# Pairing the head groups, the butterflies and x2's halves of an attention layer on Trainium2, and reordering VectorE's queue

## The chip, the cores and the metric

The kernel runs on one core of a Trainium2 chip. The core has TensorE (PE, matrix products, which read SBUF and write PSUM), VectorE (DVE), ScalarE (ACT), GpSimd (POOL, which has no way to PSUM) and SyncE (SP, which here only issues DMAs). Each engine has its own queue of instructions and works through it strictly in order; between engines only semaphores order the work, and a wait at the head of a queue holds everything behind it. The metric is the device time of the whole program in microseconds (us): the median of the runs of the kernel before is 1216.87 us (three runs, 1216.46 to 1218.15).

## The reference

```
x: (8, 1024, 512) f32; 16 heads of 32
a = layernorm(x)
Q, K, V = a@Wq.T+bq, a@Wk.T+bk, a@Wv.T+bv           (split into heads)
S = Q K^T / sqrt(32) - |i - j|, causal               (decay of the distance, -inf above the diagonal)
x = x + layernorm(softmax(S) V @ Wo.T + bo)
h = layernorm(x) @ Hadamard(512)                     (orthonormal)
q = round(h / s) * s,  s = max|h| / 7 of a row, clipped to 4 bits
x = x + layernorm(q @ ternary(W).T)
```

Because the decay is one per key of distance, a query only needs keys a short way back; the kernel computes the keys of its own 256 tokens and 64 or so before them, and checks on the chip that the inputs allow this (a flag selects a general path otherwise, which is not executed here).

## The kernel before

The 8192 tokens are cut into 32 steps of 256 (two token tiles of 128; four steps make one of the 8 sequences). The loop is a software pipeline over steps: while step s weighs its values, the queues also hold the projections of step n = s+1, the layernorm of m = s+2, the output product and the first residual of k = s-1, and the quantised product of k-1 = s-2. The order inside a step is written out by hand, once for each engine.

Large products are made in f16 with both factors split into a high and a low part (high*high + low*high + high*low, helper `split_product`, L1264). So every intermediate that goes into such a product is made twice: ACT copies it to f16 (the high part), and DVE or POOL subtracts that from the f32 value (the low part).

What the change touches:

- The 16 heads of a step are handled as four groups g = 0..3 of four heads. `keys(s, g, half)` on PE makes the scores, `exps` on ACT their exponentials, `clear_future(s, g)` on POOL (L458) zeroes what lies after the query, and `weigh(s, g)` on PE (L1380, L1385) writes into PSUM bank `ps_o[g % 2]` the weighted values (columns 0 to 255) and the sums of the weights (columns 256 to 511). Then `invert(s, g)` on ACT makes the reciprocal of the sums as exp(-ln) (L629, L631), `normalise(s, g)` on DVE multiplies and takes one Newton step in three instructions (L953, L955, L958), each waiting for the one before, into `o32[:, g % 2]`, `heads_high(s, g)` on ACT (L636) and `heads_low(s, g)` on POOL (L464) split the result into `OT`. `out_product` needs all four groups.
- `weigh(s, g)` waits until `normalise` of two groups before has read its bank. In the loop, PE weighs groups 0 and 1 in mid-step, group 2 late in the step, between the second product of V `values(n, 1)` and the third block of `scores`, and group 3 at the start of the following step, between `qk(n, 0)` and `qk(n, 1)`.
- The Hadamard transform of 512 is done as two butterflies on DVE (`fold`, L994 and L995; `fold_again`, L1003 and L1004) and a product with a 128x128 Hadamard matrix on PE (`transform`, L1407). `x2_high` (ACT, L642) and `x2_low` (DVE, L1017) split the folded rows, `turn_x2` (SP, L327) transposes both parts by DMA. All of this is done for each of the two token tiles by itself: 8 butterfly instructions, 2 + 2 splits and 4 DMA transposes a step.
- Four PSUM banks `ps_job` are taken in turn by the jobs listed in `ORDER`; a job begins when the job before it in the same bank has been read (`claim`). Thus `values(n, 1)` waits for `scale_out(k - 1, 1)` on DVE (L1041), the third and fourth block of `scores(n, ...)` (L1336, L1338) for `maxima(n, 0)` and `maxima(n, 1)` on DVE (L931), `qk(n+1, 0)` for `keep_norms(n)` (L923), `qk(n, 3)` for `qk_low_part(n, 1)` (L917) and `out_product(k, 0)` for `qk_low_part(n, 2)`.
- `residual(k)` (DVE, L987) needs the root of the variance that POOL computes in `y_root` (L446) from `y_stats` (DVE).

DVE's order in a step before, from the second `y_out` on: `y_out(k, 1)`, `y_stats(k)`, `normalise(s, 0)`, `residual(k)`, `scale_out(k-1, 0)`, the eight butterflies, `scale_out(k-1, 1)`, `z_stats(k-1)`, `x2_low(k, 0)`, `normalise(s, 1)`, `maxima(n, 0)`, `maxima(n, 1)`, `keep_norms(n)`, `z_columns(k-1)`, `x2_low(k, 1)`, `maxima(n, 2)`, `maxima(n, 3)`, `split_max(n)`, `normalise(s, 2)`, `x_stats(k)`; then of the following step `qk_low_part(n, 0)`, `normalise(k, 3)`, `qk_low_part(n, 1)`, `front_stats(m)`, `find_scale(k-1, 0)`, `front_offset(m)`, `qk_low_part(n, 2)`, `find_scale(k-1, 1)`, `qk_low_part(n, 3)`, `y_out(k, 0)`, `front_low(m)`.

Of the kernel before, what the change touches and what calls it, by code (L numbers as in the profile page):

```python
# [5 lines left out]
P = 128  # L6
# [27 lines left out]
TP = 2  # L34
# [32 lines left out]
def fast_path(nc, x, wqT, wkT, wvT, woT, bq, bk, bv, bo, wff, had16, identity, window, ident16,  # L67
# [3 lines left out]
    with ExitStack() as ctx:  # L71
# [10 lines left out]
        ps_o = [ps("o0"), ps("o1")]  # L82
# [9 lines left out]
        def score_bank(n, i):  # L92

            return bank("s", i) if n else (ps_st + ps_o)[i]
# [137 lines left out]
        x2_turned = [sem(f"x2_turned{t}") for t in range(TP)]  # L232
# [59 lines left out]
        def _(sp):  # L292
# [107 lines left out]
            for s in range(STEPS - 1):  # L400
# [14 lines left out]
                if has(k):  # L415
                    turn_x2(k, 0)
                    turn_x2(k, 1)
# [4 lines left out]
            turn_x2(last - 1, 0)  # L422
            turn_x2(last - 1, 1)
            load_res(last)
            turn_x2(last, 0)
            turn_x2(last, 1)

        @block.gpsimd
        def _(pool):
# [32 lines left out]
            def heads_low(s, g):  # L462
                pool.wait_ge(OTh_made, 4 * s + g + 1)
                nc.gpsimd.tensor_tensor(OT[s % 2][1][:, g, :], o32[:, g % 2, :], OT[s % 2][0][:, g, :],  # L464
                                        ALU.subtract).then_inc(OTl_made, 1)
# [21 lines left out]
            for s in range(STEPS - 1):  # L487
                n, m, k = s + 1, s + 2, s - 1
                square_of(n, 0)
                if has(k):  # L490
                    heads_low(k, 3)
                if has(m):
                    front_root(m)
                if has(n):
                    square_of(n, 1)
                if has(s):
                    clear_future(s, 0)
                    clear_future(s, 1)
                if has(k):
                    y_root(k)  # L500
                if has(s):
                    clear_future(s, 2)
                if has(k - 1):
                    z_root(k - 1)
                if has(s):
# [5 lines left out]
                if has(s):  # L511
                    heads_low(s, 2)

            last = STEPS - 1
            heads_low(last - 1, 3)
# [4 lines left out]
            heads_low(last, 0)  # L520
            clear_future(last, 3)
            z_root(last - 2)
            heads_low(last, 1)
            heads_low(last, 2)
            heads_low(last, 3)
# [13 lines left out]
        def _(act):  # L539
# [85 lines left out]
            def invert(s, g):  # L625

                act.wait_ge(pv_done, 4 * s + g + 1)
                until(act, o32_made, 4 * s + g - 1)
                nc.scalar.activation(inverse[:, g % 2, :], ps_o[g % 2][:, W2:D], ACT.Ln).then_inc(log_made, 1)  # L629
                act.wait_ge(log_made, 4 * s + g + 1)  # L630
                nc.scalar.activation(inverse[:, g % 2, :], inverse[:, g % 2, :], ACT.Exp,  # L631
                                     scale=-1.0).then_inc(inverse_made, 1)

            def heads_high(s, g):
                act.wait_ge(o32_made, 4 * s + g + 1)
                nc.scalar.activation(OT[s % 2][0][:, g, :], o32[:, g % 2, :],  # L636
                                     ACT.Copy).then_inc(OTh_made, 1)

            def x2_high(k, t):
                act.wait_ge(folded, 2 * (TP * k + t) + 2)  # L640
                until(act, q_turned, TP * (k - 1) + t + 1)
                nc.scalar.activation(x2h[:, t, :], folded_x[:, t, :], ACT.Copy, scale=SX).then_inc(x2h_made, 1)  # L642
# [43 lines left out]
            for s in range(STEPS - 1):  # L686
                n, m, k = s + 1, s + 2, s - 1
                qk_high_part(n, 0)
                if has(k):
                    invert(k, 3)  # L690
# [3 lines left out]
                if has(k):  # L694
                    heads_high(k, 3)
# [24 lines left out]
                invert(s, 0)  # L720
                exps(s, 2, 0)
                invert(s, 1)
# [4 lines left out]
                if has(k):  # L727
# [4 lines left out]
                exps(s, 3, 1)  # L732
                keep_v(n, 1)
# [8 lines left out]
            invert(last - 1, 3)  # L742
            heads_high(last - 1, 3)
# [9 lines left out]
            invert(last, 0)  # L753
            exps(last, 2, 0)
            keep_q(last - 2, 1)
            exps(last, 2, 1)
            exps(last, 3, 0)
            invert(last, 1)
            heads_high(last, 0)
            x2_high(last - 1, 0)  # L760
            exps(last, 3, 1)
            x2_high(last - 1, 1)
            invert(last, 2)
            heads_high(last, 1)
            norm_z(last - 2)
            invert(last, 3)
            heads_high(last, 2)
            heads_high(last, 3)
# [6 lines left out]
            x2_high(last, 0)  # L775
            x2_high(last, 1)
# [10 lines left out]
        def _(dve):  # L787
# [159 lines left out]
            def normalise(s, g):  # L947

                dve.wait_ge(inverse_made, 4 * s + g + 1)

                until(dve, OTl_made, 4 * s + g - 1)
# [133 lines left out]
            for s in range(STEPS - 1):  # L1085
                n, m, k = s + 1, s + 2, s - 1
                qk_low_part(n, 0)
                if has(k):
                    normalise(k, 3)
# [37 lines left out]
                if has(k):  # L1127
                    x2_low(k, 0)
# [4 lines left out]
                if has(k - 1):  # L1133
                    z_columns(k - 1)
# [994 lines left out]
```

## Time and profile before

| | |
|---|---|
| median of the runs shown | 1216.87 us |
| the profiled execution | 1216.83 us, span 1215.3 us |
| busy, share of the span | PE 91%, DVE 83%, weight loads 60%, ACT 58%, POOL 49% |
| granted TensorE clock, mean of the span | 0.974 |

The profile comes from one execution, 1216.83 us, of which 1215.3 us lie within the span; the other 1.5 us lie around it. The program begins with the load of the weights (until about 40 us in) and ends with a drained pipeline (from about 1110 us on); in between it is a loop whose steps take about 35 us each. Matmuls overlap one another, so a start-to-start distance says more of PE's pace than a duration does; the same is true of DVE and ACT, where the next instruction begins before the recorded end of the one before.

### The profile page before, as it was taken

To read this page: it belongs to the slowest core of one execution; us is meant where nothing else is said; L and a number is where in the kernel's file an instruction comes from. 1 tells how busy PE (TensorE), PEld (TensorE's weight loads), DVE (VectorE), ACT (ScalarE), POOL (GpSimd) and SP (SyncE) were. 2 spreads that over 40 slices of the span, in tenths; PEclk is the share of its full clock that TensorE was granted. 3 is DMA by queue.
4 is the path that set the end of the run, shared out by engine and by line. 5 is a ranking of instruction groups with operands and counts; after the bars stand their busy time and mean duration, and the time that the engine had idled before them with its cause. 6 is when DMAs were issued, how large, how long until landed. Compare 5 with 4: busy or idle time off the path is not lost.

```text
span 1215.3 us, 44904 instructions
## 1 busy us (share of the span) xinstructions
PE 1105.3 (91%) x18656; PEld 728.3 (60%) x18656; DVE 1009.3 (83%) x2558; ACT 702.9 (58%) x1494; POOL 595.7 (49%) x715
## 2 busy tenths in 40 slices
PE   5899999999999999999999999999999999999641
PEld 3566556666666666666566666666666666666320
DVE  5748998888988888899888888988888899887772
ACT  5454556665566566655666666556666655665431
POOL 2233545555454556555545555454556555545422
PEclk9999999999999999999999999999999999999875
DMA  9657565665666576656665655666576657654230
GB/s 270 150 119 143 113 138 137 155 133 132 144 124 137 138 149 145 131 132 145 124 139 137 159 135 135 137 127 134 148 139 151 135 127 151 123 115 104 67 70 37
DMA packets 204817, 161.83 MB, mean 133 GB/s; under 512 B 150432, under 2 KB 150688, under 8 KB 204512
## 3 DMA queue, kind: packets, MB, share of 16 engines
q1 hardware_dynamic: 199920, 141.86, 55.1%
q0 software_dynamic: 4688, 17.04, 3.9%
q8 instruction: 149, 2.44, 0.9%
q14 instruction: 60, 0.49, 0.1%
HBM read 40.87 MB, written 16.78 MB: 47 GB/s over the span
## 4 chain that ended last, share of the span: by engine, by line
PE 57%; DVE 31%; issue 7%; ACT 2%; SPq 1%; DMA 1%; POOL 1%; POOLq 0%; DVEq 0%; ACTq 0%
PE f_job L1264 42%; DVE f_bst L963 6%; PE f_st L1363 3%; DVE f_z L1041 3%; PE f_o L1380 2%; PE f_o L1385 2%; PE f_job L1407 2%; DVE f_o L953 2%; DVE f_inverse L955 2%; DVE f_x L987 2%; DVE f_rmax L931 2%; DVE f_folded_x L1004 2%; DVE f_y L995 2%; DVE f_y L994 2%; DVE f_small L989 1%
## 5 line engine op out<-in xcount | busy, mean ns | idle before, releaser
L458 POOL TENSOR_SCALAR_AFFINE_SELECT f_PT<-f_PT 64x512 f32<-64x512 f32 (+1 forms) x256 | 201.0, 809 | 69.6 <-ACT f_PT L618 44.2
L473 POOL TENSOR_TENSOR f_square<-f_stage 128x512 bf16<-128x512 f16 x128 | 130.9, 1044 | 135.4 <-ACT f_stage L596 119.6
L596 ACT ACTIVATE f_stage<-f_job,f_bias 128x256 f16<-128x256 f32 x256 | 106.1, 465 | 88.6 <-PE f_job L1264 81.7
L1264 PE MATMUL f_job<-f_xTh,f_wqh 128*128 128x256 f16 x512 | 140.8, 275 | 15.1 <-DVE f_wkl L794 14.3
L464 POOL TENSOR_TENSOR f_OTl<-f_o,f_OTh 128x256 f16<-128x256 f32 x128 | 86.1, 673 | 115.1 <-ACT f_OTh L636 114.5
L1264 PE MATMUL f_job<-f_xTl,f_wqh 128*128 128x256 f16 x512 | 140.1, 274 | 0.0
L1264 PE MATMUL f_job<-f_xTh,f_wql 128*128 128x256 f16 x512 | 140.1, 274 | 0.0
L1264 PE MATMUL f_job<-f_xTh,f_wkh 128*128 128x256 f16 x512 | 140.0, 273 | 0.0
L1264 PE MATMUL f_job<-f_xTh,f_wkl 128*128 128x256 f16 x512 | 139.9, 273 | 0.0
L1264 PE MATMUL f_job<-f_xTl,f_wkh 128*128 128x256 f16 x512 | 139.8, 273 | 0.0
L917 DVE SCALAR_TENSOR_TENSOR f_stage<-f_job,f_bias,f_stage 128x256 f16<-128x256 f32 x256 | 110.7, 474 | 31.7 <-ACT f_stage L596 29.7
L450 POOL TENSOR_TENSOR f_small<-f_small,f_minus_half 128x2 f32<-128x2 f32 x32 | 33.4, 1043 | 179.0 <-DVE f_small L1051 178.9
L1264 PE MATMUL f_job<-f_wvh,f_xTh 128*128 128x512 f16 x256 | 98.5, 385 | 20.1 <-DVE f_z L1041 19.3
L618 ACT ACTIVATE f_PT<-f_st 128x512 f32<-128x512 f32 x192 | 106.5, 599 | 10.0 <-PE f_st L1363 10.0
L604 ACT ACTIVATE f_V<-f_job 128x512 f32<-128x512 f32 x64 | 38.3, 598 | 112.5 <-PE f_job L1264 112.5
L1264 PE MATMUL f_job<-f_woh,f_OTh 128*128 128x512 f16 x256 | 99.2, 387 | 0.3 <-POOL f_OTl L464 0.3
L1363 PEld LDWEIGHTS f_st<-f_stacks 128*64 128x64 f16 x2432 | 67.8, 111 | 51.5 <-issue 40.0
L1264 PE MATMUL f_job<-f_woh,f_OTl 128*128 128x512 f16 x256 | 98.5, 385 | 0.0
L1264 PE MATMUL f_job<-f_wvh,f_xTl 128*128 128x512 f16 x256 | 98.3, 384 | 0.0
L1264 PE MATMUL f_job<-f_wol,f_OTh 128*128 128x512 f16 x256 | 98.3, 384 | 0.0
L1264 PE MATMUL f_job<-f_wvl,f_xTh 128*128 128x512 f16 x256 | 98.2, 384 | 0.0
L973 DVE SCALAR_TENSOR_TENSOR f_y<-f_job,f_bo_bc 128x512 f32<-128x512 f32 x64 | 44.2, 691 | 64.9 <-PE f_job L1264 64.9
(180 smaller groups left out, 3033.3 us busy)
## 6 DMA issues: line engine op xcount, KB each, us to landing
f_stacks<-f_stage SPq DMA_DIRECT2D x384, 128.0 KB
f_xin<-x SPq DMA_DIRECT2D x32, 512.0 KB, 4.7
f_x<-x SPq DMA_DIRECT2D x32, 512.0 KB, 3.9
out<-f_z POOLq DMA_DIRECT2D x32, 512.0 KB, 3.4
f_Vmix<-f_V SPq DMA_DIRECT2D x32, 256.0 KB
f_Vmix<-f_V SPq DMA_DIRECT2D x64, 128.0 KB
f_stacks<-rows_const SPq DMA_DIRECT2D x3, 512.0 KB, 9.3
f_stacks<-wqT SPq DMA_DIRECT2D x2, 512.0 KB, 5.8
```

Of the source, the lines that this page charges most:

```text
L458: nc.gpsimd.affine_select(out=d, in_=d, compare_op=ALU.is_ge, fill=0.0, base=odd * SUB, pattern=[[0, 4], [0, TP], [1, SUB]], channel_multi ...
L464: nc.gpsimd.tensor_tensor(OT[s % 2][1][:, g, :], o32[:, g % 2, :], OT[s % 2][0][:, g, :], ALU.subtract).then_inc(OTl_made, 1)
L473: nc.gpsimd.tensor_tensor(square[:, 2 * m + pair, :], h, h, ALU.mult).then_inc(squared, 1)
L596: nc.scalar.activation(stage[:, 2 * m, g, :], bank("qk", g)[:, m * W2:(m + 1) * W2], ACT.Identity, bias=bias[:, m, g:g + 1]).then_inc(qk_h ...
L604: nc.scalar.activation(V[n % 2][:, t, :], bank("v", t)[:], ACT.Copy, scale=1.0 / SQ).then_inc(v_kept, 1)
L618: nc.scalar.activation(dst, src, ACT.Exp, scale=1.0 / SS).then_inc(expd, 1)
L917: nc.vector.scalar_tensor_tensor(stage[:, 2 * m + 1, g, :], bank("qk", g)[:, m * W2:(m + 1) * W2], bias[:, m, g:g + 1], stage[:, 2 * m, g, ...
L963: note(nc.vector.bn_stats(bst[:, which, t, :], src[:, t, :]))
L973: nc.vector.scalar_tensor_tensor(y[:, t, :], bank("y", t)[:], -1.0 / (SQ * SW), bo_bc[:], ALU.mult, ALU.add).then_inc(y_made, 1)
L1041: nc.vector.tensor_tensor(z[:, t, :], bank("f", t)[:], ffscale_bc[:], ALU.mult).then_inc(z_made, 1)
L1264: mm = pe.matmul(dst, lhs[a](c), rhs[b](c), start=(n == 0), stop=(n == 3 * KC - 1))
L1363: mm = pe.matmul(ps_st[half][upper * SUB:(upper + 1) * SUB, i * W2 + q * SUB:i * W2 + (q + w) * SUB], Ks[js % 3][:, h, c * SUB:(c + 1) * SUB],
```

## The change

Groups are inverted, normalised and split two at a time: `invert`, `normalise`, `heads_high` and `heads_low` take a width w, and one instruction covers two groups (the two banks of `ps_o` become one tensor of two banks). `weigh(s, 2)` moves out of its place before the third block of scores to the following step, directly ahead of `weigh(s, 3)`. The butterflies, `x2_high`, `x2_low` and the DMA transposes of x2 cover both token tiles in one instruction. The orders of all five queues are adapted; on DVE `normalise(s, 0)` no longer stands between `y_stats` and `residual`, and groups 0 and 1 are normalised after `keep_norms` and `x2_low`. In the last step groups 2 and 3 are still handled one by one.

```diff
-        ps_o = [ps("o0"), ps("o1")]
+        ps_pair = ctx.enter_context(nc.psum_tensor("f_o", [P, 2, D], F32))
+        ps_o = [ps_pair[:, i, :] for i in range(2)]
@@ SP
-            def turn_x2(k, t):
-                sp.wait_ge(x2l_made, TP * k + t + 1)
-                until(sp, h_product, TP * (k - 1) + t + 1)
+            def turn_x2(k):
+                until(sp, h_product, TP * k)
                 for half, src in enumerate((x2h, x2l)):
-                    sp.dma_start(x2T[half][:, t], src[:, t, :], transpose=True).then_inc(x2_turned[t], 16)
+                    sp.wait_ge((x2h_made, x2l_made)[half], k + 1)
+                    sp.dma_start(x2T[half][:].rearrange("p t c n -> p (t c) n"),
+                                 src[:].rearrange("p t n -> p (t n)"), transpose=True).then_inc(x2_turned, 16)
@@ POOL
-            def heads_low(s, g):
-                pool.wait_ge(OTh_made, 4 * s + g + 1)
+            def heads_low(s, g, w):
+                pool.wait_ge(OTh_made, 4 * s + g + w)
+                nc.gpsimd.tensor_tensor(OT[s % 2][1][:, g:g + w, :], o32[:, g % 2:g % 2 + w, :],
+                                        OT[s % 2][0][:, g:g + w, :], ALU.subtract).then_inc(OTl_made, w)
...
                 square_of(n, 0)
-                    heads_low(k, 3)
+                    heads_low(k, 2, 2)
...
                     y_root(k)
-                    clear_future(s, 2)
+                clear_future(s, 2)
+                clear_future(s, 3)
                     z_root(k - 1)
-                    clear_future(s, 3)
-                    heads_low(s, 0)
-                    heads_low(s, 1)
+                heads_low(s, 0, 2)
                     finish_out(k - 1)
-                    heads_low(s, 2)
@@ ACT
-            def invert(s, g):
-                act.wait_ge(pv_done, 4 * s + g + 1)
-                until(act, o32_made, 4 * s + g - 1)
+            def invert(s, g, w):
+                slots = slice(g % 2, g % 2 + w)
+                act.wait_ge(pv_done, 4 * s + g + w)
+                until(act, o32_made, 4 * s + g + w - 2)
+                nc.scalar.activation(inverse[:, slots, :], ps_pair[:, slots, W2:D], ACT.Ln).then_inc(log_made, w)
+                act.wait_ge(log_made, 4 * s + g + w)
+                nc.scalar.activation(inverse[:, slots, :], inverse[:, slots, :], ACT.Exp,
+                                     scale=-1.0).then_inc(inverse_made, w)
...
-                    invert(k, 3)
+                    invert(k, 2, 2)
...
-                    heads_high(k, 3)
+                    heads_high(k, 2, 2)
...
-                invert(s, 0)
                 exps(s, 2, 0)
-                invert(s, 1)
+                invert(s, 0, 2)
                     keep_q(k - 1, 1)
                 exps(s, 2, 1)
                 keep_v(n, 0)
-                    x2_high(k, 0)
-                    x2_high(k, 1)
-                heads_high(s, 0)
                 exps(s, 3, 0)
                 exps(s, 3, 1)
+                    x2_high(k)
                 keep_v(n, 1)
+                heads_high(s, 0, 2)
                     norm_z(k - 1)
-                invert(s, 2)
-                heads_high(s, 1)
-                heads_high(s, 2)
@@ DVE
+            def normalise(s, g, w):
+                slots = slice(g % 2, g % 2 + w)
+                dve.wait_ge(inverse_made, 4 * s + g + w)
+                until(dve, OTl_made, 4 * s + g + w - 2)
+                heads, sums, inv = ps_pair[:, slots, 0:W2], ps_pair[:, slots, W2:D], inverse[:, slots, :]
+                nc.vector.tensor_tensor(heads, heads, inv, ALU.mult).then_inc(o_scaled, w)
+                dve.wait_ge(o_scaled, 4 * s + g + w)
+                nc.vector.tensor_tensor(inv, sums, inv, ALU.mult).then_inc(o_error, w)
+                dve.wait_ge(o_error, 4 * s + g + w)
+                nc.vector.scalar_tensor_tensor(o32[:, slots, :], inv, 2.0, heads,
+                                               ALU.subtract, ALU.mult).then_inc(o32_made, w)
...
+            def fold(k):
+                dve.wait_ge(x1_made, TP * k + TP)
+                left, right = x1[k % 2][:, :, 0:W2], x1[k % 2][:, :, W2:D]
+                nc.vector.tensor_tensor(y[:, :, 0:W2], left, right, ALU.add).then_inc(halved, 1)
+                nc.vector.tensor_tensor(y[:, :, W2:D], left, right, ALU.subtract).then_inc(halved, 1)
...
-                    normalise(k, 3)
+                    normalise(k, 2, 2)
...
-                normalise(s, 0)
                     residual(k)
                     scale_out(k - 1, 0)
-                    fold(k, 0)
-                    fold_again(k, 0)
-                    fold(k, 1)
-                    fold_again(k, 1)
+                    fold(k)
+                    fold_again(k)
                     scale_out(k - 1, 1)
                     z_stats(k - 1)
-                    x2_low(k, 0)
-                normalise(s, 1)
                 maxima(n, 0)
                 maxima(n, 1)
                 keep_norms(n)
+                    x2_low(k)
+                normalise(s, 0, 2)
                     z_columns(k - 1)
-                    x2_low(k, 1)
                 maxima(n, 2)
                 maxima(n, 3)
                 split_max(n)
-                normalise(s, 2)
                     x_stats(k)
...
-                pe.wait_ge(x2_turned[t], 32 * (k + 1))
+                pe.wait_ge(x2_turned, 32 * (k + 1))
@@ PE
                     qk(n, 0)
+                    weigh(k, 2)
                     weigh(k, 3)
                     qk(n, 1)
...
                 values(n, 1)
-                weigh(s, 2)
                 scores(n, 2)
                 scores(n, 3)
```

In the last step DVE now has `normalise(last, 0, 2)` where `normalise(last, 0)` stood (between `y_stats(last-1)` and `residual(last-1)`), and `fold(last)`, `fold_again(last)`, `x2_low(last)` over both tiles.

## Rows read from the trace of the kernel before

**Rows 1.** The page's first part, busy time of each engine:

```profile
PE 1105.3 (91%) x18656; PEld 728.3 (60%) x18656; DVE 1009.3 (83%) x2558; ACT 702.9 (58%) x1494; POOL 595.7 (49%) x715
```

**Rows 2.** Waits of PE, 100 to 1100 us: total us, times, longest:

```profile
PE f_job L1264 <- DVE f_z L1041: 18.5, 27, 1.9
PE f_job L1336 <- DVE f_rmax L931: 7.2, 13, 0.6
PE f_job L1338 <- DVE f_rmax L931: 3.9, 7, 0.6
PE f_job L1336 <- DMA f_stacks<-f_stage: 1.2, 3, 0.5
```

**Rows 3.** Timeline of PE, one step: start, us, instruction [idle before]:

```profile
409.71 0.32 PE L1380 MATMUL f_o<-f_PT,f_Vmix 128*32 128x64 f32 x8
...
410.61 0.29 PE L1380 MATMUL f_o<-f_PT,f_Vmix 128*32 128x64 f32 x8
...
419.25 0.39 PE L1264 MATMUL f_job<-f_wvh,f_xTh 128*128 128x512 f16 x1 [0.81 <-DVE f_z L1041]
...
421.94 0.32 PE L1380 MATMUL f_o<-f_PT,f_Vmix 128*32 128x64 f32 x8
...
423.58 0.19 PE L1336 MATMUL f_job<-f_stacks 107*32 107x24 f16 x1 [0.55 <-DVE f_rmax L931]
...
424.71 0.28 PE L1264 MATMUL f_job<-f_xTh,f_wqh 128*128 128x256 f16 x1
...
427.43 0.32 PE L1380 MATMUL f_o<-f_PT,f_Vmix 128*32 128x64 f32 x8
...
428.45 0.28 PE L1264 MATMUL f_job<-f_xTh,f_wqh 128*128 128x256 f16 x1
...
437.96 0.39 PE L1264 MATMUL f_job<-f_woh,f_OTh 128*128 128x512 f16 x1
...
459.54 0.28 PE L1264 MATMUL f_job<-f_xTh,f_wqh 128*128 128x256 f16 x1
```

**Rows 4.** Timeline of DVE, the same step:

```profile
409.46 0.69 DVE L973 SCALAR_TENSOR_TENSOR f_y<-f_job,f_bo_bc 128x512 f32<-128x512 f32 x1 [1.13 <-PE f_job L1264]
...
411.87 0.43 DVE L953 TENSOR_TENSOR f_o<-f_o,f_inverse 128x256 f32<-128x256 f32 x1
...
413.13 1.41 DVE L987 SCALAR_TENSOR_TENSOR f_x<-f_y,f_small,f_x 128x512 f32<-128x512 f32 x2
...
415.59 0.41 DVE L994 TENSOR_TENSOR f_y<-f_x 128x256 f32<-128x256 f32 x1
...
418.51 0.68 DVE L1041 TENSOR_TENSOR f_z<-f_job,f_ffscale_bc 128x512 f32<-128x512 f32 x1
...
422.91 1.15 DVE L931 TENSOR_REDUCE f_rmax<-f_job 128x8 f32<-128x448 f32 x2
...
424.57 0.15 DVE L1055 TENSOR_TENSOR f_small<-f_small 128x2 f32<-128x2 f32 x1
...
436.27 0.87 DVE L917 SCALAR_TENSOR_TENSOR f_stage<-f_job,f_bias,f_stage 128x256 f16<-128x256 f32 x2
```

**Rows 5.** Timeline of POOL, the root that `residual` waits for:

```profile
412.04 0.70 POOL L446 TENSOR_TENSOR f_small<-f_small,f_minus_half 128x2 f32<-128x2 f32 x1 [1.95 <-DVE f_small L979]
```

**Rows 6.** Timeline of ACT, the end of the same step:

```profile
424.95 1.52 ACT L662 ACTIVATE f_z<-f_z,f_small 128x512 f32<-128x512 f32 x2 [2.30 <-DVE f_small L1057]
```

**Rows 7.** Groups of DVE by form, 100 to 1100 us: busy us, mean ns:

```profile
L973 DVE SCALAR_TENSOR_TENSOR f_y<-f_job,f_bo_bc 128x512 f32<-128x512 f32 x56 | 38.7, 691 | 48.0 <-PE f_job L1264 48.0
...
L1041 DVE TENSOR_TENSOR f_z<-f_job,f_ffscale_bc 128x512 f32<-128x512 f32 x56 | 38.1, 680 | 0.0
```

**Rows 8.** Timeline of SP's queue, the regrouping of Q and K:

```profile
440.23 9.66 SPq L353 DMA_DIRECT2D f_stacks<-f_stage  x12
```

**Rows 9.** Timeline of PE and of DVE in the drained end:

```profile
1161.85 0.59 PE L1264 MATMUL f_job<-f_woh,f_OTh 128*128 128x512 f16 x1 [0.32 <-POOL f_OTl L464]
...
1184.08 0.16 DVE L1026 SCALAR_TENSOR_TENSOR f_job<-f_x_mv,f_job 128x1 f32<-128x1 f32 x1
```

More of the change, by code:

```diff
@@ L231, in fast_path @@
         folded = sem("folded")
-        x2_turned = [sem(f"x2_turned{t}") for t in range(TP)]
+        x2_turned = sem("x2_turned")
         x2h_made = sem("x2h_made")
@@ L415, in _ @@
                 if has(k):
[L416 to L417 removed]
+                    turn_x2(k)
             last = STEPS - 1
@@ L519, in _ @@
             clear_future(last, 2)
-            heads_low(last, 0)
+            z_root(last - 2)
             clear_future(last, 3)
[L522 to L525, printed above, removed]
+            heads_low(last, 0, 2)
+            heads_low(last, 2, 1)
+            heads_low(last, 3, 1)
             finish_out(last - 2)
@@ L752, in _ @@
             level(last - 2, 1)
-            invert(last, 0)
             exps(last, 2, 0)
+            invert(last, 0, 2)
             keep_q(last - 2, 1)
@@ L757, in _ @@
             exps(last, 3, 0)
-            invert(last, 1)
-            heads_high(last, 0)
-            x2_high(last - 1, 0)
             exps(last, 3, 1)
-            x2_high(last - 1, 1)
-            invert(last, 2)
-            heads_high(last, 1)
+            heads_high(last, 0, 2)
+            x2_high(last - 1)
+            invert(last, 2, 1)
             norm_z(last - 2)
-            invert(last, 3)
-            heads_high(last, 2)
-            heads_high(last, 3)
+            invert(last, 3, 1)
+            heads_high(last, 2, 1)
+            heads_high(last, 3, 1)
             round_levels(last - 1, 0)
@@ L774, in _ @@
             keep_q(last - 1, 1)
-            x2_high(last, 0)
-            x2_high(last, 1)
+            x2_high(last)
             norm_z(last - 1)
@@ L1144, in _ @@
             last = STEPS - 1
-            normalise(last - 1, 3)
+            normalise(last - 1, 2, 2)
             find_scale(last - 2, 0)
@@ L1150, in _ @@
             y_stats(last - 1)
-            normalise(last, 0)
+            normalise(last, 0, 2)
             residual(last - 1)
@@ L1154, in _ @@
             scale_out(last - 2, 1)
-            fold(last - 1, 0)
-            fold_again(last - 1, 0)
+            fold(last - 1)
+            fold_again(last - 1)
             z_stats(last - 2)
-            fold(last - 1, 1)
-            fold_again(last - 1, 1)
-            x2_low(last - 1, 0)
-            normalise(last, 1)
+            x2_low(last - 1)
             z_columns(last - 2)
-            x2_low(last - 1, 1)
-            normalise(last, 2)
-            normalise(last, 3)
+            normalise(last, 2, 1)
+            normalise(last, 3, 1)
             x_stats(last - 1)
@@ L1172, in _ @@
             residual(last)
-            fold(last, 0)
-            fold_again(last, 0)
-            fold(last, 1)
-            fold_again(last, 1)
-            x2_low(last, 0)
+            fold(last)
+            fold_again(last)
+            x2_low(last)
             scale_out(last - 1, 0)
             scale_out(last - 1, 1)
-            x2_low(last, 1)
             z_stats(last - 1)
@@ L1491, in _ @@
             last = STEPS - 1
+            weigh(last - 1, 2)
             weigh(last - 1, 3)
```

86 lines of the change are left out of this document (28 added, 58 removed).

## The prediction

> **What bounds the kernel now.** The first view is busy time: PE 91% of the span, DVE 83%, the others far behind [rows 1]. PE is the candidate, but its share is an average, so the next view is who makes PE wait. In 1000 us of the loop it waited 29.6 us for DVE, at three places: before `values(n, 1)` for `scale_out` (18.5), before the third and fourth block of scores for `maxima` (7.2 and 3.9); DMAs hardly count [rows 2]. The timeline of one step shows where: 0.81 us at 419.25 and 0.55 at 423.58 [rows 3]. The step lasts 459.54 - 424.71 = 34.83 us [rows 3]. So the loop is bound by PE's own work, with DVE late at two points of each step. DVE in turn waits for PE once, at the second `y_out` (1.13 us at 409.46, [rows 4]). The step is therefore two rings that touch: PE's queue, and DVE's queue from `y_out(k, 1)` round to `qk_low_part(n, 2)`, which frees the bank of the next output product (PE at 437.96). I work out both for the new order; the longer one is the new step.
>
> **DVE's ring.** Before, `y_out(k, 1)` at 409.46 to `qk_low_part(n, 2)` at 436.27 is 26.81 us [rows 4].
> - Residual: `normalise(s, 0)` costs 413.13 - 411.87 = 1.26 us there [rows 4]. It goes from this place, but it covered POOL's root, which runs 412.04 to 412.74 [rows 5]. Residual can start at about 412.80, so only 0.33 us is won; DVE stands idle 0.9 us in its place.
> - Butterflies: eight take 418.51 - 415.59 = 2.92 us [rows 4]. A joined one has 512 elements a partition; the nearest row is 680 ns, for 128x512 in f32 [rows 7], and as a next instruction starts some 0.08 us before a recorded end (413.13 + 1.41 is 414.54, and eight butterflies of 0.41 take 2.92, less than 3.3), I take 0.60 start to start. Four of these and one wait of 0.11: 2.51, 0.41 won. Bound: if the joined one costs as two (0.67), 0.13 is won, not 0.41.
> - Normalising: four singles of 1.26 are 5.04 us a step. A pair is three instructions on 2x256 elements that wait for one another. The trace has no instruction over two banks; the nearest row is 691 ns for 512 elements from one bank [rows 7], the other end is two singles, 0.85 for each. With 0.69: 0.72 + 0.72 + 0.60 = 2.04 a pair, 4.08 a step. Since the first single is already counted under residual, three singles (3.78) become two pairs (4.08): +0.30. With the other end +1.26.
> - `x2_low`, 2 x 0.60 against one of about 1.22: nothing. An idle 0.17 ahead of `qk_low_part(n, 1)`, where ACT was late, is used up.
> - Sum: -0.33 - 0.41 + 0.30 - 0.17 = -0.61, so 26.20. The `qk_low` itself takes 0.87 [rows 4]; from the output product at 437.96 round to the next `y_out(k, 1)` are 34.83 - (437.96 - 409.46) = 6.33 [rows 3, 4], pure PE work. Ring: 26.20 + 0.87 + 0.05 + 6.33 = 33.45 us.
>
> **PE's ring.** Its two waits go as causes: 34.83 - 0.81 - 0.55. `weigh(s, 2)` moves. Alone between f16 products a weigh occupies 423.58 - 0.55 - 421.94 = 1.09 and 428.45 - 427.43 = 1.02; the first of two in a row takes 410.61 - 409.71 = 0.90 [rows 3]. Two together are then 0.90 + 1.02 = 1.92, not 2.11: 0.19 won. That makes 33.28. Now what is late next:
> - `scale_out(k-1, 1)` starts 0.33 + 0.41 earlier, 417.77, and ends at 418.50; PE is free at 419.25 - 0.81 = 418.44. 0.06 is left of the first wait.
> - `values(n, 1)` takes 421.94 - 419.25 = 2.69, then come the two score blocks, at 421.19. DVE from `scale_out` to `maxima` took 422.91 - 418.51 = 4.40, of which a single normalise and one `x2_low` (1.86) now come later: `maxima` start at 420.31 and end at 420.9 and 421.4; the blocks want them at 421.2 and 421.7. No wait. `keep_norms` follows (two maxima and it: 424.57 - 422.91 = 1.66), done at 422.05; `qk(n+1, 0)` wants it at 421.19 + 1.13 = 422.32 (424.71 - 423.58) [rows 3, 4]. No wait, by 0.3.
> - The new wait: `weigh(s, 2)` needs the whole of `normalise(s, 0, 2)`, that stands behind `x2_low`: 421.97 + 1.22 + 2.14 = 425.3. PE is there at 422.32 + 2.72 = 425.04 (427.43 - 424.71). It waits 0.3, and behind it in PE's queue are `weigh(s, 3)` and all of `qk(n, 1)`. With two-singles pairs it is 0.8.
> - PE's ring: 33.28 + 0.06 + 0.30 = 33.64, just longer than DVE's 33.45. `qk(n, 3)` finds its bank free by 0.6, the output product by 0.2.
>
> **ACT, POOL, SP.** ACT now has `heads_high(s, 0, 2)`, which waits for the pair, ahead of `norm_z` and of the next step's `qk_high_part`. `norm_z` starts at about 425.9 instead of 424.95 and takes 1.5 [rows 6]; the high part is ready by 428.2 and DVE gets to `qk_low_part(n, 0)` only at 428.7, since pair, `z_columns`, two maxima, `split_max` and `x_stats` stand before it. Nothing, as long as the pair is not over 0.5 late. POOL loses work. SP issues two long transposes for four short ones, sooner: its next waiter, `max_rows`, is not held by them. One thing does tighten: `front_offset` gives ACT its third and fourth jobs, so `qk_low_part(n, 3)`, from which the regrouping of Q and K starts, comes only 0.61 earlier a step while PE comes 1.2 earlier. The twelve transfers take up to 9.66 us to issue [rows 8], and in three steps the scores already waited for them [rows 2]. The masks of group 1 lose as much. I put both at 4 us in all, between 0 and 0.55 x 28 = 15.
>
> **The sum.** Per step of the kind shown, 34.83 - 33.64 = 1.2. Over the loop, by the waits of PE: 29.6 removed, 28 x 0.19 = 5.3 from the neighbouring weighings; new, 0.36 in three of four steps (in the first step of a sequence PE has more work and arrives later), 21 x 0.36 = 7.6, and the 4 us: 29.6 + 5.3 - 7.6 - 4 = 23.3 us. The drained end: `out_product(last, 0)` at 1161.85 hangs on the last low part [rows 9], which is as early as before; but in the last butterflies both tiles must pass ACT and DVE before `find_scale` (1184.08, [rows 9]), about 0.7 later. With less idling earlier, +0.5, between -2 and +2. 23.3 - 0.5 = 22.8. The profiled execution took 1216.83 us (span 1215.3 and 1.5 around it), as the median of the runs, 1216.87: 1216.83 - 22.8 = **1194 us**.
>
> **A rule against it.** DVE is busy 83% and leaves PE gaps of 0.81 and 0.55 us [rows 1, 3]. The Trainium skill (Perfetto Trace Analysis, Optimizing Scalar/DVE Operations) says that where such an engine isn't saturated but makes others wait, breaking instructions up may let work finish sooner. The change joins them. What this would do here is the third rival.
>
> **The rivals.**
> 1. PE runs without new waits. For it: both margins that I find negative are 0.06 and 0.3 us, the size of my errors. Against it: three engines are within 0.3 us of each other. 29.6 + 5.3 = 35 us: 1182.
> 2. Transfers and masks take what DVE gives. For it: the DMA row in [rows 2], and PE coming 0.55 us sooner on them. Against: 25 of 28 steps show no such wait. 15 us in place of 4: 1205.
> 3. The joined halves come late: PE, that needs half, waits for the whole pair. For it: the pair ends 0.9 after a single would. Then `weigh(s, 2)` waits 1.2 and not 0.3 in each step: 28 x 0.9 = 25, all the gain: 1219 at most, 1217 with the others' slack.
> 4. Slower: a joined instruction costs as its two parts. Place: DVE's ring. Price: pairs +0.96, butterflies +0.28, ACT's joined logarithm and exponential +0.35, together 1.59 us a step; 33.45 + 1.59 = 35.04, over 34.83 by 0.21, for 28 steps 6 us: 1223. It decides from 34.83 - 33.45 = 1.38 us of excess on. Against it: 512 elements cost 691 ns and not twice 430 [rows 4, 7]; for it: no row spans two banks.
>
> **Chances.** Forecast 0.60 (1186 to 1201), first rival 0.12, second 0.16, third 0.04, fourth 0.08. A measurement of this kernel tells some 0.2% (2.4 us) from no change. Faster 0.88, same 0.04, slower 0.08. The range takes in the second rival up to 1212 and the half of the first: 1183 to 1212.
>
> **What would show it.** In the profile after: steps of about 33.7 us; PE's wait for `scale_out` nearly gone, none for `maxima`, a new one of 0.3 us ahead of `weigh(s, 2)` on DVE's normalise; pairs of 0.69 us and butterflies of 0.68; an idle 0.9 us of DVE ahead of residual; the DMA wait of the scores grown. Wrong it would be if pairs take over 0.8 us, if PE waits over 1 us for DVE at the weighing, or if the output product's bank is late by more than 0.3.

## The result, and the profile after

The changed kernel takes 1245.57 us (median of four, 1244.21 to 1247.67) against 1217.41 us for the kernel before on the same chip (1216.46 to 1218.15): ratio 1.0229, 95% interval 1.0212 to 1.0245 (given so for every run below, each against the kernel before as timed beside it). It is 28 us slower where 23 us less were forecast, and outside the range.

The page of the changed kernel, busy time and the chain that ended last (line numbers are those of the changed kernel from here on):

```profile
PE 1115.3 (90%) x18625; PEld 732.8 (59%) x18656; DVE 1019.4 (82%) x2209; ACT 675.7 (54%) x1273; POOL 586.4 (47%) x652
...
DVE 60%; PE 15%; issue 10%; ACT 10%; POOL 3%; DMA 1%; SPq 1%; DVEq 0%; POOLq 0%; ACTq 0%
```

DVE runs 349 instructions fewer than before and is yet busy 10 us longer [rows 1]; DVE holds 60% of the chain, where it held 31% before. Waits of PE in the changed kernel, 100 to 1100 us (total us, times, longest), which answer to [rows 2]:

```profile
PE f_o L1350 <- DVE f_o L941: 13.7, 27, 1.0
PE f_job L1234 <- DVE f_stage L900: 12.7, 20, 0.6
PE f_job L1306 <- DVE f_rmax L914: 3.6, 8, 0.5
PE f_job L1306 <- DMA f_stacks<-f_stage: 2.9, 5, 1.1
PE f_job L1308 <- DVE f_rmax L914: 2.1, 4, 0.5
PE f_job L1306 <- issue: 1.9, 1, 1.9
PE f_job L1308 <- DMA f_stacks<-f_stage: 1.3, 2, 0.7
PE f_job L1234 <- DVE f_z L1024: 1.1, 2, 0.5
```

The wait for `scale_out` (18.5) is down to 1.1 and the new one ahead of `weigh(s, 2)` is there, as forecast; not forecast is the one before `qk(n, 3)`, for `qk_low_part(n, 1)`. So DVE is late in its long stretch from `y_out(k, 1)` on. Timeline of DVE in one step of the changed kernel, which answers to [rows 4]:

```profile
735.90 0.69 DVE L956 SCALAR_TENSOR_TENSOR f_y<-f_job,f_bo_bc 128x512 f32<-128x512 f32 x1 [0.91 <-PE f_job L1234]
...
741.22 0.68 DVE L977 TENSOR_TENSOR f_y<-f_x 128x512 f32<-128x512 f32 x1
741.81 1.14 DVE L978 TENSOR_TENSOR f_y<-f_x 128x512 f32<-128x512 f32 x1
742.99 0.69 DVE L986 TENSOR_TENSOR f_folded_x<-f_y 128x512 f32<-128x512 f32 x1
...
744.80 0.58 DVE L1029 SCALAR_TENSOR_TENSOR f_small<-f_x_mv,f_small 128x2 f32<-128x2 f32 x1
745.41 0.53 DVE L1031 SCALAR_TENSOR_TENSOR f_small<-f_small 128x2 f32<-128x2 f32 x1
...
754.09 0.61 DVE L923 TENSOR_SCALAR f_mh<-f_rmax 128x32 f16<-128x32 f32 x1
754.74 1.21 DVE L926 SCALAR_TENSOR_TENSOR f_mh<-f_rmax,f_mh 128x32 f16<-128x32 f32 x1
755.87 1.27 DVE L992 BATCH_NORM_STATS2 f_bst<-f_x 128x6 f32<-128x512 f32 x2
...
760.30 0.87 DVE L900 SCALAR_TENSOR_TENSOR f_stage<-f_job,f_bias,f_stage 128x256 f16<-128x256 f32 x2
...
771.94 0.69 DVE L956 SCALAR_TENSOR_TENSOR f_y<-f_job,f_bo_bc 128x512 f32<-128x512 f32 x1 [0.98 <-PE f_job L1234]
```

The step is 771.94 - 735.90 = 36.04 us, 1.21 more than before. (Every fourth step, the first of a sequence, takes 35.5 us in both kernels.) Two instructions on 2 elements a partition take 0.5 us, one on 32 takes 1.21, and of two butterflies alike the second takes 1.14. The timeline of POOL in the same stretch says beside what:

```profile
740.59 1.82 POOL L457 TENSOR_SCALAR_AFFINE_SELECT f_PT<-f_PT 64x512 f32<-64x512 f32 x2 [1.42 <-ACT f_PT L609]
744.66 1.28 POOL L457 TENSOR_SCALAR_AFFINE_SELECT f_PT<-f_PT 64x512 f32<-64x512 f32 x2 [2.25 <-ACT f_PT L609]
...
753.49 1.17 POOL L463 TENSOR_TENSOR f_OTl<-f_o,f_OTh 128x512 f16<-128x512 f32 x1 [5.10 <-ACT f_OTh L628]
754.62 2.50 POOL L478 TENSOR_TENSOR f_z<-f_z,f_x 128x512 f32<-128x512 f32 x2
```

Each long one lies beside a POOL instruction. The small ones end where POOL's ends: L923 at 754.70, POOL's low part at 754.66; L1031 at 745.94, the two masks at 745.94. The butterfly L978, which has more work of its own, ends at 742.95, 0.54 after the masks at 742.41. The butterfly before it, L977, has two inputs in SBUF as well and lies beside the same masks, and keeps its 0.68. There it is the mask that is long, 1.20 us, while the pair of masks at 744.66 takes 1.28 for both; the second mask of the first pair alone:

```profile
741.21 1.20 POOL L457 TENSOR_SCALAR_AFFINE_SELECT f_PT<-f_PT 128x512 f32<-128x512 f32 x1
```

`BATCH_NORM_STATS2` at 755.87, beside POOL's sum, keeps its time, as do the instructions with an operand in PSUM. The groups of DVE by form, 100 to 1100 us, give it for the whole loop (busy us, mean ns); first the kernel before, then the changed one, where L923 and L926 are before's L940 and L943, and L1029 and L1031 its L1046 and L1048:

```profile
L943 DVE SCALAR_TENSOR_TENSOR f_mh<-f_rmax,f_mh 128x32 f16<-128x32 f32 x29 | 5.6, 192 | 1.0
L940 DVE TENSOR_SCALAR f_mh<-f_rmax 128x32 f16<-128x32 f32 x29 | 5.0, 173 | 0.0
L1048 DVE SCALAR_TENSOR_TENSOR f_small<-f_small 128x2 f32<-128x2 f32 x28 | 4.5, 160 | 1.0
L1046 DVE SCALAR_TENSOR_TENSOR f_small<-f_x_mv,f_small 128x2 f32<-128x2 f32 x28 | 4.2, 149 | 0.0
```

```profile
L939 DVE TENSOR_TENSOR f_inverse<-f_o,f_inverse 128x512 f32<-128x512 f32 x56 | 38.7, 692 | 6.2 <-DVE f_o L937 0.5
...
L926 DVE SCALAR_TENSOR_TENSOR f_mh<-f_rmax,f_mh 128x32 f16<-128x32 f32 x28 | 32.7, 1167 | 1.0
L978 DVE TENSOR_TENSOR f_y<-f_x 128x512 f32<-128x512 f32 x28 | 30.1, 1076 | 0.0
L986 DVE TENSOR_TENSOR f_folded_x<-f_y 128x512 f32<-128x512 f32 x28 | 22.7, 811 | 1.0
L977 DVE TENSOR_TENSOR f_y<-f_x 128x512 f32<-128x512 f32 x29 | 19.7, 680 | 0.0
...
L923 DVE TENSOR_SCALAR f_mh<-f_rmax 128x32 f16<-128x32 f32 x28 | 17.2, 614 | 0.0
L1031 DVE SCALAR_TENSOR_TENSOR f_small<-f_small 128x2 f32<-128x2 f32 x27 | 11.7, 433 | 0.9
L1029 DVE SCALAR_TENSOR_TENSOR f_small<-f_x_mv,f_small 128x2 f32<-128x2 f32 x27 | 10.8, 400 | 0.0
```

I call this a hold below: a DVE instruction that reads two tensors in SBUF, or goes from SBUF to SBUF as `TENSOR_SCALAR`, doesn't get on while an instruction of POOL runs (or, as with L977, the one of POOL doesn't get on beside it). In this step the holds are 0.46 + 0.43 + 0.37 + 0.44 + 1.02 = 2.72 us over the unheld times (0.68, 0.15, 0.16, 0.17, 0.19), for L978, L1029, L1031, L923 and L926 in this order.

### The profile page after: what moved, and what is told of

The parts are those of the page before. It is cut to its first block, busy times and chain, and to the rows that moved or that the text cites. A ratio compares the mean times of both kernels' runs of the same rounds, so it can differ in the third digit from the quotient of the medians.

```text
span 1242.3 us, 44245 instructions
## 1 busy us (share of the span) xinstructions
PE 1115.3 (90%) x18625; PEld 732.8 (59%) x18656; DVE 1019.4 (82%) x2209; ACT 675.7 (54%) x1273; POOL 586.4 (47%) x652
## 4 chain that ended last, share of the span: by engine, by line
DVE 60%; PE 15%; issue 10%; ACT 10%; POOL 3%; DMA 1%; SPq 1%; DVEq 0%; POOLq 0%; ACTq 0%
PE f_job L1234 11%; DVE f_bst L946 6%; DVE f_rmax L914 4%; DVE f_stage L900 3%; DVE f_inverse L939 3%; DVE f_o L941 3%; DVE f_o L937 3%; DVE f_bst L992 3%; DVE f_fst L876 3%; DVE f_mh L926 3%; DVE f_x2l L1000 3%; DVE f_y L978 2%; ACT f_xin L570 2%; DVE f_x L970 2%; DVE f_folded_x L986 2%
## 5 line engine op out<-in xcount | busy, mean ns | idle before, releaser
L457 POOL TENSOR_SCALAR_AFFINE_SELECT f_PT<-f_PT 64x512 f32<-64x512 f32 (+1 forms) x256 | 210.0, 844 | 137.5 <-ACT f_PT L609 92.7
L463 POOL TENSOR_TENSOR f_OTl<-f_o,f_OTh 128x512 f16<-128x512 f32 (+1 forms) x65 | 74.5, 1146 | 181.3 <-ACT f_OTh L628 181.3
L628 ACT ACTIVATE f_OTh<-f_o 128x512 f16<-128x512 f32 (+1 forms) x65 | 40.5, 624 | 169.4 <-DVE f_o L941 169.3
L1333 PE MATMUL f_st<-f_stacks 128*64 128x128 f16 (+1 forms) x2432 | 96.6, 215 | 8.9 <-DMA f_stacks<-f_mrow 3.3
```

The lines of the kernel that those rows point to most:

```text
L457: nc.gpsimd.affine_select(out=d, in_=d, compare_op=ALU.is_ge, fill=0.0, base=odd * SUB, pattern=[[0, 4], [0, TP], [1, SUB]], channel_multi ...
L463: nc.gpsimd.tensor_tensor(OT[s % 2][1][:, g:g + w, :], o32[:, g % 2:g % 2 + w, :], OT[s % 2][0][:, g:g + w, :], ALU.subtract).then_inc(OTl ...
L628: nc.scalar.activation(OT[s % 2][0][:, g:g + w, :], o32[:, g % 2:g % 2 + w, :], ACT.Copy).then_inc(OTh_made, w)
L1333: mm = pe.matmul(ps_st[half][upper * SUB:(upper + 1) * SUB, i * W2 + q * SUB:i * W2 + (q + w) * SUB], Ks[js % 3][:, h, c * SUB:(c + 1) * SUB],
```

## The experiments

Theory A is the hold. Its rivals: the pairs themselves cost the time, or the joined halves do by coming late, or the new orders of the queues alone.

**POOL's work cut short, in both kernels.** The masks cover 2 columns of 64, and the squares, the low parts of the heads and the last sums 8 columns each. The rest of these is left out; waits and orders stay.

```diff
-                    d = tiles[0:P if odd else SUB, :, :, odd * SUB:(odd + 1) * SUB]
+                    d = tiles[0:P if odd else SUB, :, :, odd * SUB:odd * SUB + 2]
...
-                nc.gpsimd.tensor_tensor(OT[s % 2][1][:, g:g + w, :], o32[:, g % 2:g % 2 + w, :],
+                nc.gpsimd.tensor_tensor(OT[s % 2][1][:, g:g + w, 0:8], o32[:, g % 2:g % 2 + w, 0:8],
...
```

> The changed kernel, in which GpSimd's masks, low parts of the heads, squares and last sums cover only a few columns each (it leaves out the rest of them; all instructions, waits and orders stay). Theory A (VectorE is held while GpSimd reads and writes SBUF, and the new order puts VectorE's instructions with two inputs from SBUF beside GpSimd's): the second butterfly L978 falls from 1.14 us to 0.68, the low part of the maxima from 1.20 to 0.19, the two small ones of the z statistics from 0.57 and 0.53 to 0.15, the step from 35.9 to about 34, the time to 1190 to 1200. Theory B (the loss is the new order of waits, above all weigh 2 waiting for the joined normalise): these durations may change, but the changed kernel stays over 20 us slower than the kernel before with the same shortening.

> The kernel before with the same shortening of GpSimd's instructions (same parts left out). Theory A: little is to be won, since only L989 (0.61 us) and L899 (0.50 us) are long beside GpSimd in the kernel before: 0.5 to 0.8 us less in a step, 1195 to 1205, so as fast as the changed kernel with the shortening or slower. Theory B: at least 20 us faster than the changed kernel with the shortening.

Measured: changed kernel 1183.97 us (0.9727 of before, 0.9697 to 0.9757), kernel before 1200.51 (0.9867, 0.9839 to 0.9895). The groups of the changed kernel so cut:

```profile
L982 DVE TENSOR_TENSOR f_y<-f_x 128x512 f32<-128x512 f32 x30 | 20.5, 684 | 0.0
...
L930 DVE SCALAR_TENSOR_TENSOR f_mh<-f_rmax,f_mh 128x32 f16<-128x32 f32 x30 | 5.8, 193 | 1.0
L927 DVE TENSOR_SCALAR f_mh<-f_rmax 128x32 f16<-128x32 f32 x30 | 5.2, 172 | 0.0
...
L1035 DVE SCALAR_TENSOR_TENSOR f_small<-f_small 128x2 f32<-128x2 f32 x29 | 4.7, 160 | 1.0
...
L1033 DVE SCALAR_TENSOR_TENSOR f_small<-f_x_mv,f_small 128x2 f32<-128x2 f32 x29 | 4.4, 151 | 0.0
```

All five are back at their own time, and 62 us go, where the same cut gives the kernel before only 17. Without POOL's neighbourhood the change is 16.5 us faster, near the 22.8 forecast. The pairs, the late halves and the orders are all still in this kernel, so none of them by itself is what makes the change slower. The cut also brings POOL's results sooner, though; that the holds and not POOL's lateness cost the time is seen from the kernel with two waits in POOL's queue further down, where POOL's work comes later and nothing is left out.

**Half of the cut each**: only the masks short, or only the low parts of the heads and the last sums (the edits above, one at a time).

> The changed kernel with GpSimd's masks alone cut to two columns of 64 (the rest of the masking is left out). Theory A (VectorE is held by GpSimd's instruction beside it): L978 back to 0.68 us (-0.47), L986 to 0.69 (-0.1), L1029 and L1031 to 0.15 and 0.16 (-0.5); the low part of the maxima stays at 1.2 us. 1.0 to 1.1 us less a step, 28 steps: 1246 - 29 = 1217. If it were the number of GpSimd's instructions or their waits, not their length: no change.

> The changed kernel with only GpSimd's low parts of the heads and the last sums cut to eight columns (the rest of both left out), masks and squares whole. Theory A: L923 back from 0.61 to 0.17 us and L926 from 1.17 to 0.19, together 1.4 us less a step; L978, L1029 and L1031 stay long: 1246 - 39 = 1207. The gains of this one and of the one with short masks should add up to those of both, near 1184. If weigh 2 waiting for the joined normalise were the cause: no change.

Measured 1214.76 us (0.9964, 0.9949 to 0.998) and 1212.14 (0.9946, 0.9926 to 0.9966). With short masks L978, L1029 and L1031 fell to 685, 150 and 162 ns and L926 stayed at 1172; in the other it was the reverse (192 for L926, 1111 for the butterfly). 31 + 33 = 64 us, against 62 for both with the squares cut as well: each hold belongs to one neighbour, and they add.

**One part of the change alone.** The kernel before with only the butterflies, x2's parts and the transposes joined; and the changed kernel with these apart again, so only with the pairs, the moved weighing and the orders.

```diff
-                    fold(k, 0)
-                    fold_again(k, 0)
-                    fold(k, 1)
-                    fold_again(k, 1)
+                    fold(k)
+                    fold_again(k)
...
-                    x2_low(k, 0)
...
-                    x2_low(k, 1)
+                    x2_low(k)
```

> The kernel before with only the butterflies, x2's two parts and its transposes over both token tiles, x2_low at the place of the second one; head groups, weighings and all other orders as before. Theory A: the butterflies stand behind GpSimd's masks as before, so each takes 0.68 us; TensorE's waits fall by 0.3 us before values and by most of 0.4 before the scores, 28 steps: 1217 - 19 = 1198. If the joined instructions themselves are what costs: slower than 1217, towards 1230.

> The changed kernel with the butterflies, x2's parts and their transposes apart for the two tiles again, at the same places of the queues; the head groups in pairs, the third weighing beside the fourth, and the orders stay. Nothing is left out. Theory A: the holds at the maxima's split and at z's statistics come with the pairs and the orders, not with the joined instructions, so this part alone is slower than the kernel before: by sums, 1245.6 less the -26 us of the joined part, 1271 us; taking one butterfly's hold of 0.46 us a step as gone with the joining, 1257. Range 1250 to 1275. Rival: only both parts together are slow (the joined instructions let GpSimd's run beside others): 1215 to 1225 us.

Measured 1191.40 us (0.9781, 0.9761 to 0.9801) and 1254.49 (1.0301, 1.0284 to 1.0318). The joined part is worth 26 us by itself and is faster than both kernels; in it all four butterflies take 676 to 692 ns and the split of the maxima stays short. The other part costs 37 us. The two don't add: 37 - 26 would be 11, and the whole change costs 28, so beside the pairs the joining is worth only 1254.49 - 1245.57 = 9 us. The groups of the kernel with the other part alone:

```profile
L931 DVE SCALAR_TENSOR_TENSOR f_mh<-f_rmax,f_mh 128x32 f16<-128x32 f32 x28 | 32.7, 1168 | 1.0
L983 DVE TENSOR_TENSOR f_y<-f_x 128x256 f32<-128x256 f32 x56 | 32.0, 571 | 0.0
L992 DVE TENSOR_TENSOR f_folded_x<-f_y 128x256 f32<-128x256 f32 x56 | 27.5, 491 | 0.0
...
L928 DVE TENSOR_SCALAR f_mh<-f_rmax 128x32 f16<-128x32 f32 x28 | 17.2, 613 | 0.0
```

The second halves of its butterflies are long too (L983 571 ns against 414 of L982). So it is the pairs and their order, which put POOL's low part and last sums beside `split_max` and the masks beside the butterflies, that bring the holds.

**Moving POOL's work, nothing left out.** First the last sums behind the next step's `front_root`.

```diff
                 if has(m):
                     front_root(m)
+                if has(k - 2):
+                    finish_out(k - 2)
...
                 heads_low(s, 0, 2)
-                if has(k - 1):
-                    finish_out(k - 1)
```

> The changed kernel with one move on GpSimd: the last sums and the store of a step (finish_out) go from behind heads_low(s, 0, 2) to behind front_root of the following step. Nothing is left out. Theory A: the low part of the maxima on VectorE falls from 1.20 us to 0.19, which shortens VectorE's ring by about 1 us a step: 1246 - 27 = 1219. Theory B: no change, 1246 within 3 us, since weigh 2 and 3 on TensorE are released before that instruction.

A miss: 1254.10 us (1.0294, 1.0271 to 1.0317). L927, the held one, did fall to 192 ns. But the sums now lay beside the front offset, and what waits for them moved too; group of DVE, and a wait of SP's queue:

```profile
L887 DVE SCALAR_TENSOR_TENSOR f_small<-f_small 128x2 f32<-128x2 f32 x28 | 24.6, 878 | 0.0
```

```profile
SPq L338 <- POOL f_z L478: 133.7, 26, 5.4
```

`load_res`, ahead of later transfers in SP's queue, waited 5 us a step for the sums, and PE's waits for the regrouped Q and K ahead of the scores rose from 4.2 us to 23.7 + 10.2 = 33.9. Then two waits in POOL's queue and the masks of groups 2 and 3 behind the root of z:

```diff
-                clear_future(s, 2)
-                clear_future(s, 3)
                 if has(k - 1):
                     z_root(k - 1)
+                if has(k):
+                    pool.wait_ge(x2l_made, k + 1)
+                clear_future(s, 2)
+                clear_future(s, 3)
+                pool.wait_ge(max_parts, n + 1)
                 heads_low(s, 0, 2)
```

> The changed kernel, nothing left out, with three instructions of GpSimd held back by waits on VectorE: the masks of groups 2 and 3 come behind z_root and wait for x2_low(k), heads_low(s, 0, 2) waits for the low part of the maxima. Theory A: all five stretched instructions of VectorE get short again (0.68, 0.69, 0.15, 0.16, 0.19 us), VectorE's ring falls below TensorE's, and the time comes to what was forecast for the change, 1190 to 1200. If more waiting on GpSimd can only cost (it delays masks that weigh 2 needs): 1246 or more.

Measured 1214.13 us (0.9952, 0.9936 to 0.9968), 31 less than the change, but not the 1190 to 1200 expected. All five are short again, and new ones are long: `z_columns` (L1041) with 468 ns against 154, and above all L885, the small `TENSOR_SCALAR` behind the statistics of the front layernorm. Timeline of DVE, then of POOL, in that kernel:

```profile
710.64 1.23 DVE L885 TENSOR_SCALAR f_small<-f_small 128x2 f32<-128x2 f32 x1
```

```profile
708.68 2.04 POOL L472 TENSOR_TENSOR f_square<-f_stage 128x512 bf16<-128x512 f16 x2
710.68 1.15 POOL L463 TENSOR_TENSOR f_OTl<-f_o,f_OTh 128x512 f16<-128x512 f32 x1
```

L885 takes 1084 ns in the mean, against 169 in the changed kernel. To see whether that was the rest, the squares were moved off it:

```diff
-                square_of(n, 0)
                 if has(k):
                     heads_low(k, 2, 2)
                 if has(m):
                     front_root(m)
+                if has(k - 1):
+                    pool.wait_ge(qinv_made, TP * k)
+                square_of(n, 0)
                 square_of(n, 1)
```

> The kernel with GpSimd's waits (1214.1 us), in which GpSimd besides takes the square sums of a step only after the third group pair's low part, the front root and VectorE's second scale of the quantiser. Nothing is left out. Theory A (VectorE's instructions with two inputs in SBUF, or from SBUF to SBUF, end with GpSimd's running one; the 1.08 us of the tensor_scalar in front_stats, against 0.17, are such a hold, and the last 30 us of that kernel): that instruction falls back under 0.25 us, no other group rises by more than 0.2 us in its mean, and the time is 1185 to 1197 us. Rival: a further instruction takes the hold (the candidates are the low part of x, 1.30 us, and the small ones of the quantiser), then 1205 to 1220 us. Rival B (GpSimd's neighbourhood plays no part, only the orders do): 1214.

Measured 1204.91 us (0.9899, 0.9882 to 0.9915): 9 less, not 17 to 29; the rival, that a further instruction takes the hold, had 1205 to 1220. L887 (the same instruction) is back at 168 ns, but the low part of x (L897) rose from 1.32 to 1.72 us, and PE waited 14.4 us for masks. I took these for the masks of groups 2 and 3 and let them go at once (the wait for `x2l_made` taken out):

> The kernel with the square sums late (1204.9 us), in which the masks of blocks 2 and 3 follow the root of z at once and no longer wait for x2's low part; so it is the changed kernel with nothing left out, only GpSimd's queue in another order with two waits. There TensorE waited 14.4 us in all for the masks. Theory A: the masks then lie beside the maxima and the norms, which read PSUM and aren't held, TensorE's wait for them goes, x2's low part is held once by what is left of one mask (at most 0.6 us), and the time is 1190 to 1200 us, which is what was forecast for the change. Rival: x2's low part is held by a whole mask and z's columns and the pair behind it come late in turn: 1203 to 1212 us.

A miss in both respects: 1224.98 us (1.0058, 1.004 to 1.0077). The wait for masks stayed, 13.9 us; it is in mid-step at `weigh(s, 0)`, behind the late squares. x2's low part went from 1214 to 2070 ns, and PE's wait for the pair behind it from 1.2 us to 18.0:

```profile
L1003 DVE SCALAR_TENSOR_TENSOR f_x2l<-f_folded_x,f_x2h 128x1024 f16<-128x1024 f32 x29 | 60.0, 2070 | 0.0
```

**The fast version further.** In the kernel with only the joined part, y's offset (L984) took 564 ns beside a mask. It was moved behind `z_columns`; in another kernel the mask was moved instead, behind the root of z.

> The kernel with joined tiles (1191) and one more move on VectorE: the offset of y (L984, two elements a partition, 0.56 us beside GpSimd's masks) goes from behind residual to behind z_columns, where GpSimd is idle. Theory A: 0.15 us there, 0.4 us less ahead of scale_out, for which TensorE still waits 9 us in 16 steps: 1191 - 8 = 1183. If the instruction is long for another reason than its neighbour: no change.

> The kernel before with only the butterflies and x2's parts joined over both tiles (1191.4 us), and the third block's mask moved behind the root of z on GpSimd. Nothing is left out. Theory A: the y offset falls from 0.56 us to 0.16, the butterflies stay at 0.68, and because TensorE there waits for VectorE only 9 us in all (f_z), the time falls by no more than that: 1182 to 1188 us. Rival: the masks, now 2.5 us in a row, hold x2's low part or z's columns and TensorE's third weighing waits for the mask: 1192 to 1200 us.

Measured 1190.19 us (0.9762, 0.9744 to 0.978) and 1204.12 (0.989, 0.9873 to 0.9906). The first is no change clear of noise where 8 us were expected, the second 13 us slower than the joined part alone. In the first the offset fell to 159 ns and the butterflies behind it, unheld until then (676 and 679), rose to 809 and 972: the hold passed to the next instruction in the queue that can be held. In the second they stayed at 680, but `z_columns` went to 401 and 618 ns, and PE now stood before the third weighing for its mask, in nearly every step; waits of PE, 100 to 1100 us:

```profile
PE f_o L1364 <- POOL f_PT L456: 26.6, 28, 1.2
```

## Why the prediction was wrong

- **The step that failed** is DVE's ring, "Sum: -0.33 - 0.41 + 0.30 - 0.17 = -0.61, so 26.20", and beside it "POOL loses work", priced at nothing. I took DVE's durations from the kernel before as its own. They were durations beside other neighbours, and the change moves both queues against each other. From `y_out(k, 1)` to the end of `qk_low_part(n, 1)` is 761.17 - 735.90 = 25.27 us against 432.15 + 0.88 - 409.46 = 23.57 before: 1.7 longer, not 0.6 shorter. Of the 2.3 between, the holds are 2.72, the pairs' mis-sizing 0.30, and y's offset, which was held before (609 ns in the mean) and no longer is (185), gives 0.42 back; the rest of -0.3 lies in small idles. That the holds are the cause, and not only beside it, the cut of POOL's work and the kernel with the two waits in POOL's queue (31 us back with nothing left out) showed together.
- The Trainium skill states this rule (SBUF — State Buffer, Who interferes with whom): DVE's second input from SBUF comes through the read interface that it shares with GpSimd, so an instruction with two SBUF inputs contends with a GpSimd one that reads SBUF, and so does a `tensor_scalar` in a 2-port mode; whoever starts first keeps it for the whole instruction. The trace agrees: 1167 ns for 192 at L926, a mask of 1.20 us beside L977, nothing at `BATCH_NORM_STATS2` (675 to 685 ns) and at instructions with a PSUM operand. I had not weighed it, though the trace of before had it as well, in y's offset.
- **PE's waits.** `scale_out` gone (1.1 us left): right. The new wait ahead of the weighing: right in place, 0.5 us a step and not 0.3. "No wait" at the maxima: wrong, 5.7 us. `qk(n, 3)` free by 0.6: wrong, it waits in 20 steps for 12.7 us. All three are DVE late by the holds: with POOL cut short only the wait at the weighing is left, 8.3 us, and 0.5 for `scale_out`.
- **Pairs.** 688 to 692 ns each, as taken; the term was mis-sized in the gaps. Start to start is 0.79, 0.80, 0.60, thus 2.19 a pair and not 2.04.
- **Butterflies.** 0.60 start to start for the first (741.22 to 741.81): right wherever POOL leaves them alone. The fourth rival, that joined ones cost as two, is out.
- **Residual.** DVE's idle ahead of it was forecast at 0.9: 22.9 us in 28 steps, 0.82. Right.
- **Transfers and masks.** 4 us forecast, (2.9 + 1.3) - (1.2 + 0.5) = 2.5 measured at the scores (0.5 us in two further places at L1338 before, which [rows 2] doesn't show). Right for the transfers; for masks PE has no wait in the loop's list.
- **The drained end** was put at +0.5 us, between -2 and +2: wrong. From the second `y_out` of the last step but two to that of the last step it is 1169.31 - 1109.23 = 60.08 us before and 1196.18 - 1129.67 = 66.51 us in the changed kernel. Of the 27 us between the two spans, 6.4 arise here, and 21 in the 28 steps ahead (1109.23 - 127.39 = 981.84 us against 1129.67 - 126.83 = 1002.84). In the last step POOL's new order has a mask of the fourth group behind `z_root(last - 2)`, and PE waits for it:

```profile
1182.58 0.44 PE L1350 MATMUL f_o<-f_PT,f_Vmix 128*32 128x64 f32 x8 [8.82 <-POOL f_PT L457]
```

In the kernel before PE's one wait for a mask in the last steps is 0.8 us. With POOL's work cut short the wait is still 8.0 us, yet the stretch takes only 60.7, so how much of the 6.4 is this order's was not settled.
- **Breaking up instead of joining**, the rule I weighed against the change: joining was not what cost. The joined part alone gave 26 us, and 9 beside the pairs.

What stays open is an order of POOL's queue for the changed kernel in which nothing is held: the best without anything left out is 1204.9 us. Nor was it settled why the sums of PE's listed waits move by less than the time does: PE waits for DVE 29.6 us in the loop of the kernel before (1217.4) and 33.2 in that of the changed one (1245.6). A part lies in the score matmuls, which this list doesn't show: over the whole run they are busy for 93.7 + 88.9 = 182.6 us against 171.8 before, with mean durations only 1 ns apart, and in the changed kernel the weight loads ahead of them wait for ACT's exponentials (PEld is PE's weight load; 100 to 1100 us):

```profile
PEld f_st L1333 <- ACT f_PT L609: 16.5, 62, 0.4
```

In the kernel before they have no such wait. The forecast had "Nothing" for ACT; no run moved ACT's queue alone, so what this costs isn't shown.

## What to carry to other kernels

A duration from a trace holds for its neighbours of then. When a queue is reordered, lay VectorE's and GpSimd's timelines over one another in the new order, and look for every VectorE instruction with two SBUF inputs, or a `TENSOR_SCALAR` from SBUF to SBUF, however small, that falls beside GpSimd's work; put reductions, statistics and PSUM readers there (beside POOL's low part the reduction L921 kept its 186 ns). Check the queue of the last steps by itself, where its order is written out apart. Taking one instruction out of the way hands the hold to the next: what has to move is the overlap, with all that waits for the moved work.

## What the runs showed of the hardware

- What a hold costs isn't bounded by the size of the held instruction: 2 elements a partition took 1.08 us in the mean for 0.17 (L885 in the kernel with the two waits in POOL's queue, beside one low part).
- It can last over the border of two POOL instructions. In the kernel with the masks let go, x2's low part started at 702.38, between masks that started at 702.13 and 702.75, and ended at 704.48; with its own 1.21 us it got on only at about 703.3, one whole mask later. The last mask, started at 703.37, took 1.63 us instead of 0.66: the hold works in both directions, and here each engine lost about 0.9.
- Beside a running POOL instruction these kept their time: `BATCH_NORM_STATS2` (one input in SBUF, 675 ns at L992), `TENSOR_REDUCE` (186 ns at L921), and the `TENSOR_TENSOR` L1024 with one input in PSUM (0.68 us at 740.61).
- DVE instructions that each wait for the one before start 0.10 us after the recorded end of the one before at 512 elements, and 0.03 to 0.04 at 256 (0.46 start to start for 0.42 to 0.43).
